# A decoder layer with routed experts: routed rows and shares of experts 9 to 64 are loaded from ScalarE's queue, four experts ahead, in place of SyncE's queue, eight ahead

## The reference

```python
x = x + attn(layernorm(x))                # 16 heads, causal, rope
x = x + xattn(layernorm(x), ctx_2048)     # 16 heads, int8 fake-quant of x, wq, o, wp
x = x + ffn(layernorm(x))                 # 64 experts, 8 per token
# ffn, for 4096 tokens xf:
scores = softmax(xf @ router_w.T); topk_w, topk_idx = top_k(scores, 8); topk_w /= topk_w.sum()
xb[e] = up to 128 rows of xf sent to expert e
yb[e] = (silu(xb[e] @ w_gate[e]) * (xb[e] @ w_up[e])) @ w_down[e]     # 512 -> 192 -> 512
out[token] += yb[its slot] * topk_w
```

## Time and profile before

| what | value |
|---|---|
| median of 3 runs | 1580.34 us (1577.61 to 1582.3) |
| the profiled execution | 1569.49 us |
| its span | 1567.4 us |
| PE busy | 1405.6 us (90%) |
| DVE busy | 1166.1 us (74%) |
| ACT busy | 970.7 us (62%) |
| POOL busy | 673.5 us (43%) |
| hardware DMA queue (SP's) | 120768 packets, 157.27 MB |
| software DMA queue (POOL's) | 38912 packets, 37.87 MB |

### The profile page before, as it was taken

The page is one execution under the profiler, slowest core; times in us unless marked ns, Lnnn a source line. Parts: engine busy times, 40 slices in busy tenths (PEclk is TensorE's granted clock), DMA queues, the critical chain, the costliest instruction groups (busy, mean ns, idle before and its releaser), DMA issues.

```text
span 1567.4 us, 35601 instructions
## 1 busy us (share of the span) xinstructions
PE 1405.6 (90%) x10963; PEld 1062.5 (68%) x10996; DVE 1166.1 (74%) x3111; ACT 970.7 (62%) x3345; POOL 673.5 (43%) x654
## 2 busy tenths in 40 slices
PE   3499999999999999999999999999719888888895
PEld 2367777777777777777777777777516555655573
DVE  5768888999899998999989999988624444444453
ACT  3357777777777777777777777777604333333342
POOL 0011454444544434535345453444443554555556
PEclk9799999999999999999999999999859999999998
DMA  9681233222211110111111011100597999999964
GB/s 294 255 312 42 97 136 119 99 105 88 90 40 38 41 34 27 27 34 35 39 27 27 27 34 41 33 21 22 187 328 220 284 266 279 283 273 281 265 100 50
DMA packets 159737, 195.80 MB, mean 125 GB/s; under 512 B 39541, under 2 KB 121845, under 8 KB 159680
## 3 DMA queue, kind: packets, MB, share of 16 engines
q1 hardware_dynamic: 120768, 157.27, 30.6%
q0 software_dynamic: 38912, 37.87, 11.9%
HBM read 127.60 MB, written 130.29 MB: 165 GB/s over the span
## 4 chain that ended last, share of the span: by engine, by line
PE 66%; DMA 23%; issue 5%; DVE 3%; ACT 1%; POOL 1%; SPq 1%; POOLq 0%; DVEq 0%
PE bank L502 34%; DMA out<-x,slots 20%; PE bank L527 7%; PE bank L484 7%; PE bank L520 5%; PE bank L534 4%; PE bank L508 3%; PE bank L540 2%; PE bank L515 2%; DMA x_in<-in_x 1%; PE bank L489 1%; DMA wide_b<-in_xkT_w 1%; POOL routed L1753 1%; ACT probs L966 1%; DMA probsT<-in_oT_w 1%
## 5 line engine op out<-in xcount | busy, mean ns | idle before, releaser
L966 ACT ACTIVATE probs<-bank,small 128x128 f32<-128x128 f32 x1024 | 362.1, 377 | 48.3 <-DVE small L1270 45.0
L1753 POOL DMA_INDIRECT routed<-row,slots x248 | 253.8, 1023 | 133.5 <-issue 73.7
L1822 POOL DMA_INDIRECT out<-x,slots x128 | 198.9, 1554 | 194.8 <-DMA out<-x,slots 140.5
L1718 POOL TENSOR_TENSOR small<-small,half 128x1 f32<-128x1 f32 x96 | 54.6, 569 | 523.6 <-DVE small L1242 523.6
L966 ACT ACTIVATION_READ_ACCUMULATOR probs<-bank,small 128x1 f32 x1024 | 220.7, 216 | 0.0
L960 ACT ACTIVATE probsT<-bank 128x512 f32<-128x512 f32 x256 | 143.9, 610 | 88.5 <-PE bank L527 88.5
L1270 DVE TENSOR_REDUCE small<-bank 128x4 f32<-128x512 f32 x256 | 166.7, 682 | 33.8 <-PE bank L520 33.8
L527 PE MATMUL bank<-idf,probs 128*128 128x128 f32 x1024 | 146.8, 277 | 2.7 <-ACT probs L966 2.4
L1673 DVE TENSOR_SCALAR slots<-pairs 128x1 uint32<-128x1 f32 x128 | 13.7, 149 | 172.0 <-DMA out<-x,slots 168.4
L527 PEld LDWEIGHTS bank<-idf,probs 128*128 128x128 f32 x1024 | 121.7, 144 | 27.0 <-DVE probs L1279 3.8
L1200 ACT ACTIVATE xn<-bank 128x192 f32<-128x192 f32 x64 | 21.3, 332 | 147.4 <-PE bank L906 147.4
(11 more groups left out here) (242 smaller groups left out, 3838.4 us busy)
## 6 DMA issues: line engine op xcount, KB each, us to landing
w_gate_up<-in_w_gate SPq DMA_DIRECT2D x128, 192.0 KB, 3.6
w_gate_up<-in_w_up SPq DMA_DIRECT2D x128, 192.0 KB, 3.9
w_down<-in_w_down SPq DMA_DIRECT2D x128, 192.0 KB, 4.3
routed<-empty_row SPq DMA_DIRECT2D x4, 5120.0 KB, 22.0
x_in<-in_x SPq DMA_DIRECT2D x32, 256.0 KB, 2.6
ctx_sb<-in_ctxT_in SPq DMA_DIRECT2D x32, 256.0 KB, 3.0
x_res<-in_x SPq DMA_DIRECT2D x32, 256.0 KB, 2.5
out<-x SPq DMA_DIRECT2D x32, 256.0 KB, 2.0
```

Of the source, the lines that this page charges most:

```text
L966: last = act.activation(probs[:, g, j * P:(j + 1) * P], bank[:, b, j * P:(j + 1) * P], ACT.Exp, bias=negated[:, h:h + 1], **({"accum_out": ...
L1753: pool.indirect_dma_start(routed, bass.IndirectOffsetOnAxis(ap=slots_of(m)[:, k:k + 1], axis=0), row_of(m)[:, :], None, bounds_check=SLOTS ...
L1822: pool.indirect_dma_start(out.rearrange("b p (h c) -> (b p h) c", h=2), bass.IndirectOffsetOnAxis(ap=place_of[k % 2][:, half_:half_ + 1], ...
```

## The change

SP no longer loads rows and pairs after those of experts 1 to 8; its loop keeps the wait and the weights. ACT gets a `load_rows` of its own. In its step n, for n from 5 to 60, between down_hi(n-2) and copy_rows(n), it waits until expert n-4 is scaled and then loads rows and pairs of expert n+4 into the buffers of place (k+4) mod 8. The last round of 16 steps is written out, since its last four steps load nothing; ACT's loop runs two rounds in place of three.

```diff
--- before.py
+++ after.py
@@ -467,11 +467,7 @@
             with sp.Fori(0, E // RING - 1) as i:
                 for k in range(RING):
                     until(sp, m_y, sp.snap(i * (2 * RING) + nth(k + 1, 2, 2)))
-                    load_rows(sp.snap(i * RING + (NROWS + k)), k % NROWS)
                     load_weights(sp.snap(i * RING + (RING + k)), k)
-            for n in range(E - NROWS + 1, E + 1):
-                until(sp, m_y, nth(n - NROWS, 2, 2))
-                load_rows(n - 1, (n - 1) % NROWS)
             for half_ in range(2):
                 sp.wait_ge(s_added[half_], 16 * E)
 
@@ -1210,19 +1206,32 @@
                 until(act, m_hT, n)
                 copy(hiddenT_hi[k % 2][:, :], bank[:, 4 + k % 2, 0:2 * P], m_hThi)
 
+            def load_rows(e, k):
+                act.dma_start(rows[k][:, :], routed_e[e][:, 0:D]).then_inc(s_rows[k], 16)
+                act.dma_start(pair[k][:, :], pair_of(e)).then_inc(s_rows[k], 16)
+
+            def rows_ahead(n, k):
+
+                until(act, m_y, nth(n - 4, 2, 2))
+                load_rows(n + 3 if isinstance(n, int) else act.snap(n + 3), (k + 4) % NROWS)
+
             def step(n, k, j):
                 if not isinstance(n, int) or n >= 3:
                     silu(n - 2, (k - 2) % RING)
                     down_hi(n - 2, (k - 2) % RING, j + 1 if k >= 2 else j)
+                if not isinstance(n, int) or 5 <= n <= E - 4:
+                    rows_ahead(n, k)
                 copy_rows(n, k)
                 if not isinstance(n, int) or n >= 3:
                     hidden_hi(n - 2, (k - 2) % RING)
 
             for k in range(RING):
                 step(k + 1, k, 0)
-            with act.Fori(1, E // RING) as j:
+            with act.Fori(1, E // RING - 1) as j:
                 for k in range(RING):
                     step(j * RING + (k + 1), k, j)
+            for k in range(RING):
+                step((E // RING - 1) * RING + k + 1, k, E // RING - 1)
             for n in (E - 1, E):
                 silu(n, (n - 1) % RING)
                 down_hi(n, (n - 1) % RING, E // RING)
```

## The result

The changed kernel takes 1592.93 us (median of 5 runs, 1590.01 to 1595.31) against 1577.72 us for the kernel before (5 runs, 1577.34 to 1582.3). The ratio is 1.0089, 95% interval 1.0073 to 1.0106: slower by 0.9%, some 14 us (15 us between the medians). The forecast was "no change", 1580.5 us, in a range of 1571 to 1593. The range holds the measured time by 0.07 us, and only because its top was lent by a rival whose mechanism the runs do not bear out: that is luck, and the forecast of no change was wrong.

A forecast was written before the change was run, and what follows sets the result against it. Scatter-add landings under full DMA engines bound the 48 loaded experts, PE the tail. Terms of 0 for SP, lead, ScalarE and contention left the profiled 1569.5 us; the forecast was the runs' median, 1580.5 us, range 1571 to 1593.

The forecast's parts named there:

- The bound: Expert stage: scatter-add landings chain under full DMA engines, 6.2 us per expert over 48; then PE-bound, 4.75 us each.
- SP's two DMAs: SP's queue: row and pair loads leave, 1.12 us less issue per expert, weights begin earlier; cost and gain 0.
- The DMA engines' term: Loaded steps: same bytes from three queues; taken as 0, bounds 9 us less to 32 us more.
- Lead of the rows: Row loads ahead of PE's transposes: nearly the same moment as before, 16 us of cover, cost 0.
- ScalarE: ScalarE's added wait and two DMA issues in 56 of 64 steps: slack absorbs them, cost 0; upper bound 5.5 us.
- Rival D: ScalarE's two DMA issues cost over 1.7 us, making PE-bound steps late: 1586 to 1592 us; chance 0.04.
- Rival B: Third queue's rows and weights take turns ahead of scatter-adds, lengthening landing: 10 to 16 us slower, 1590 to 1596; chance 0.26.
- Rival C: Two issuers fill the DMA dips, mean share up by up to 3%: 9 us faster, 1571.5 us; chance 0.20.

The follow-up runs named there:

- e8: Kernel before, with the 288 weight DMAs of experts 17 to 64 spread evenly over 56 steps in place of 48, SP's loop written out; ratio 1.0101.
- e2: Kernel before, with SP issuing the same DMAs in one queue but weights ahead of rows and pairs; ratio 1.0038.
- e3: Kernel before, with only the 1 KB pair load issued from ScalarE; SP loads rows, then weights; ratio 1.0083.
- e4: Kernel before, with only the 256 KB row load issued from ScalarE; SP loads the pair, then weights; ratio 1.0003.
- e1: Kernel before, with ScalarE's added wait for m_y but none of its DMAs; SP still loads rows, pairs and weights; ratio 0.9989.
- e15: Kernel before, with the pair load ahead of the row load, both on SP ahead of the weights; ratio 1.0034.
- e16: Changed kernel, with no pair load per expert: SP loads pairs of eight experts at once, once in eight steps, SP's loop written out; ratio 1.0181.

## Why the prediction was right or wrong

**The bound: half right.** The chain, the waits and the place of the change in it were read rightly, and the time did change in the landing of the scatter-adds, where the text said to look. "The DMA engines are full" was true as an observation, and wrong as a reason: e8 took a seventh of the weight load away and the step did not shrink (6.29 us against 6.14 to 6.27).

**SP's two DMAs: looked at in one place only.** "Cost and gain 0" looked at the weights' use, 16 experts later, where indeed nothing waits. It did not look at what else the weights' start decides. SP's wait for m_y went from 75.7 us in 42 waits to this:

```profile
SPq L335 <- DVE x L1688: 151.6, 46, 6.2
```

1.8 us per wait became 3.3. The text named that longer wait, forecast as 1.1 us, and called it free. It is the time in which SP has nothing left to issue. The weights' earlier start has no fixed price, though: e2 starts them right after m_y and loses 0.4%, e3 at 0.70 us and loses 0.8%, e4 at 0.79 us and loses nothing. What SP's share of the loss is, apart from ScalarE's, stays open.

**The DMA engines' term: the step that failed, 0 for 0.32 us per expert.** "I take 0 ... total work, not its order, sets the period" is the sentence that the result contradicts: work per expert stayed at 6.3 to 6.4 us, and where and in what order the loads are issued changed the period from 6.14 to 6.46 us, as the adds' landing went from 5.2 to 5.6 us. 48 x 0.32 = 15 us, inside the bounds of -9 and +32. The choice of 0 between them rested on "total work sets the period", which e8 contradicts. Why this placement lengthens the landing is open, as said above.

**Lead of the rows: right.** No engine waits for rows or pairs in the loaded steps.

**ScalarE: right, with smaller sizes.** e1 shows that the wait is free. The pair of issues takes 1.12 us in the step shown (1309.11 to about 1310.23), the price I took. hidden_hi comes 1.89 us after m_y; I had 1.77. In the PE-bound tail I forecast a slip of 0.33 us. The changed kernel's tail:

```profile
1519.56 0.46 ACTq L1211 DMA_DIRECT2D pairs<-routed  x1
...
1520.70 0.60 ACT L956 ACTIVATE x_res<-bank 128x512 f32<-128x512 f32 x1 [0.79 <-PE bank L894]
...
1521.19 0.38 ACT L956 ACTIVATE hiddenT_hi<-bank 128x256 fp32r<-128x256 f32 x1
...
1522.98 0.19 PEld L914 LDWEIGHTS bank<-attT_hi,hiddenT_hi 128*128 128x128 f32 x1
...
1524.25 0.41 ACT L1202 ACTIVATE cT_hi<-w_down 128x256 fp32r<-128x256 f32 x1
```

There is none: the DMAs are issued under the running down_hi copy, and copy_rows still waits 0.79 us for PE's transposes, as in the earlier trace rows. The tail step is 4.75 us as before (1524.25 to 1529.00 for the next). Rival D did not happen.

**Rival B: its marks, not its mechanism.** It gave 1590 to 1596 us, landing over 5.3 us and share below 1.03; measured were 1592.9, 5.6 and 0.97. But it put the price on the rows' bytes taking turns in a third queue. With those bytes there and only the pair back on SP (e4) nothing is lost, and with one queue and another order (e2, e15) some of it is. An add that only had more competitors would be expected to find the engines busier, not idle. The chance of 0.26 sat on the right side for a reason that the runs do not bear out.

**Rival C** asked for fuller engines from two issuers; the share fell. The Trainium skill's rule (DMA: Bandwidth & Descriptors, "Issuing engines are not separate DMA queues") agrees with e4: rows from another issuer brought no bandwidth, 272 GB/s as in e1. The prediction took its 0 as agreeing with that rule; what was lost here is no issue time but the overlap of the adds' data with the start of the loads.

## What to carry to other kernels

When one event releases all transfers of a step, and a chain of latencies gives the step its length, the engines can run dry between the last data of one step and the first of the next; a busy share near 1 can hide that by luck of phase, so fold the share by distance from that event before calling a transfer's order or queue free. Shortening the issue of such loads was no gain here, and cost. And take load away in one run before you call a resource the bound.

## What the runs showed of the hardware

- After the engines had run dry, a step's first weight packets moved 1.0 us after their issue (1309.11 to 1310.1) and the DMA share was full after 2.4 us (1311.5).
- A scatter-add of 128 rows of 1 KB lands in 3.8 us with no weight loads beside it (before), in 5.2 us (before) to 6.0 us (e16) beside them, and in 5.4 us also with a seventh fewer of them (e8).
- A load of 128 pairs of 8 bytes, 1 KB in all, shifts the kernel by 0.3% to 0.8% by its place (e15, e3), and taking it out of the loop, with SP's loop written out, made the changed kernel another 0.9% slower (e16 1.0181 against 1.0089).
- The 128 packets of such a load take 10 ns each, 0.08 us of the 16 engines in all (before and after), so its effect is not its own time.
